# The order of the matmuls in the projection of a graph attention layer: block by block, or the blocks in turn

## The reference

```python
adj = dep_type_matrix != 0
dep_emb = dep_emb_table[dep_type_matrix]
hi_t = einsum('bid,de->bie', h, W1_w[:HID])[:, :, None, :] + einsum('bijd,de->bije', dep_emb, W1_w[HID:]) + W1_b
hj_t = einsum('bjd,de->bje', h, W2_w[:HID])[:, None, :, :] + einsum('bijd,de->bije', dep_emb, W2_w[HID:]) + W2_b
masked = where(adj, sum(hi_t * hj_t, axis=-1), NEG)
A = softmax(masked, axis=2)
h_syn = relu(einsum('bij,bjd->bid', A, h) @ gcn_w + gcn_b)
out = layernorm(x + h_syn @ Wo_w + Wo_b)
```

## Time and profile before

| | |
|---|---|
| time, median of 3 runs | 412.35 us (411.92 to 412.51) |
| span of the profiled execution | 410.8 us |
| PE busy | 397.4 us (97%) |
| PE, weight loads | 366.1 us (89%) |
| DVE busy | 319.2 us (78%) |
| POOL busy | 196.6 us (48%) |
| ACT busy | 130.8 us (32%) |
| DMA queue with the loads and stores | 33.9% of the 16 engines' time |

### The profile page before, as it was taken

How to read it: one execution, slowest core, us unless ns; L and a number is a source line. 1 busy time by engine, 2 the same in 40 slices (tenths; PEclk the granted TensorE clock), 3 DMA queues, 4 the chain that set the end, 5 groups by cost and what they waited for, 6 DMA issues and landing times.

```text
span 410.8 us, 8012 instructions
## 1 busy us (share of the span) xinstructions
PE 397.4 (97%) x2867; PEld 366.1 (89%) x2867; DVE 319.2 (78%) x640; ACT 130.8 (32%) x272; POOL 196.6 (48%) x159
## 2 busy tenths in 40 slices
PE   8999999999999999999999999999999999999971
PEld 4888998989999898999989899998989899898971
DVE  1544796988979698897979969697997979698764
ACT  1624233142323314232331333233142323314151
POOL 0290628165392816438173564717265292816052
PEclk9999999999999999999999999999999999999996
DMA  7903016070433507053070715216070342504022
GB/s 243 343 17 91 1 47 199 0 243 2 142 100 90 152 0 243 0 157 86 12 231 0 196 46 167 76 37 205 0 230 12 123 120 81 161 0 153 1 79 79
DMA packets 34476, 42.78 MB, mean 104 GB/s; under 512 B 9824, under 2 KB 28640, under 8 KB 34464
## 3 DMA queue, kind: packets, MB, share of 16 engines
q1 hardware_dynamic: 34320, 42.62, 33.9%
q10 hardware_dynamic: 144, 0.00, 0.0%
HBM read 30.03 MB, written 12.58 MB: 104 GB/s over the span
## 4 chain that ended last, share of the span: by engine, by line
PE 85%; DVE 9%; POOL 2%; issue 2%; DMA 1%; SPq 0%; DVEq 0%; POOLq 0%
PE bank L365 16%; PE bank L366 16%; PE bank L367 16%; PE bank L429 10%; PE bank L444 6%; PE bank L450 6%; PE bank L445 6%; PE bank L389 5%; DVE srow L763 2%; DVE rel L773 2%; PE bank L418 2%; PE bank L472 2%; DVE y_sb L696 1%; DVE stats L701 1%; DMA w1t_sb<-in_w_t_dram 1%
## 5 line engine op out<-in xcount | busy, mean ns | idle before, releaser
L971 POOL TENSOR_TENSOR veps<-mv,eps_sb 128x2 f32<-128x2 f32 (+1 forms) x33 | 8.6, 260 | 136.7 <-DVE mv L710 136.7
L688 DVE COPY hg_sb<-bank 128x385 f32<-128x385 f32 x64 | 35.6, 557 | 49.0 <-PE bank L367 47.2
L963 POOL TENSOR_TENSOR x_sb<-x_sb,wob_sb 128x1536 f32<-128x1536 f32 x16 | 58.3, 3648 | 28.5 <-DMA x_sb<-in_x_dram 28.5
L818 DVE CAST hs_hi<-hs_sb 128x512 fp32r<-128x512 f32 x48 | 66.6, 1412 | 1.8 <-ACT hs_sb L659 1.8
L444 PE MATMUL bank<-wo_hi,hs_hi 128*128 128x384 f32 x192 | 66.6, 347 | 0.0
L450 PE MATMUL bank<-wo_hi,hs_lo 128*128 128x384 f32 x192 | 65.2, 340 | 1.5 <-POOL hs_lo L1010 1.5
L365 PE MATMUL bank<-gcn_hi,xt_hi 128*128 128x386 f32 x192 | 66.5, 346 | 0.0
L445 PE MATMUL bank<-wo_lo,hs_hi 128*128 128x384 f32 x192 | 65.1, 339 | 0.0
L367 PE MATMUL bank<-gcn_hi,xt_lo 128*128 128x386 f32 x192 | 64.9, 338 | 0.0
L366 PE MATMUL bank<-gcn_lo,xt_hi 128*128 128x386 f32 x192 | 64.8, 338 | 0.0
L954 POOL TENSOR_TENSOR xt_lo<-xt_sb,xt_hi 128x1536 fp32r<-128x1536 f32 x15 | 52.2, 3483 | 16.2 <-ACT xt_hi L605 11.2
(11 more groups left out here) (77 smaller groups left out, 640.1 us busy)
## 6 DMA issues: line engine op xcount, KB each, us to landing
x_sb<-in_x_dram SPq DMA_DIRECT2D x16, 768.0 KB, 4.6
xt_sb<-in_x_t_dram SPq DMA_DIRECT2D x15, 768.0 KB, 5.5
out_dram<-y_sb SPq DMA_DIRECT2D x30, 384.0 KB, 3.4
adj_sb<-in_adj_dram SPq DMA_DIRECT2D x16, 128.0 KB, 5.2
xt_sb<-in_x_t_dram SPq DMA_DIRECT2D x2, 384.0 KB, 5.9
out_dram<-y_sb SPq DMA_DIRECT2D x4, 192.0 KB, 2.0
w2t_sb<-in_w_t_dram SPq DMA_DIRECT2D x3, 192.0 KB, 3.6
w1t_sb<-in_w_t_dram SPq DMA_DIRECT2D x3, 192.0 KB, 3.7
```

The source lines that it names most:

```text
L818: dve.tensor_copy(hs_hi[:, f, :], hs_sb[:, f, :]).then_inc(hshi, 1)
L963: pool.tensor_tensor(x_sb[:, slot], x_sb[:, slot], wob_sb[:].rearrange("p (o n) -> p o n", o=1).to_broadcast([P, PAIRS, HID]), ALU.add).th ...
```

## The change

In `proj` the block f becomes the innermost loop. All waits for `hg_ready` come ahead of the first matmul. Each of the three kinds of product (high-high, low x, low M) of a chunk c is done for the three blocks in turn, so that neighbouring matmuls write to banks 0, 1, 2, 0, 1, 2. The number of matmuls, their operands and sizes, and the order in which the terms of one block are added stay. The counts of `proj_mm` come with the last three matmuls.

```diff
@@ -369,14 +369,15 @@
             def proj(g, par):
                 pe.wait_ge(xlo, g + 1)
                 for f in range(C):
-
-
                     pe.wait_ge(hg_ready, PAIRS if isinstance(g, int) and g == 1 else PAIRS * g + min(f + 1, 2))
-                    fs = slice(f * P, (f + 1) * P)
-                    for c in range(C):
-                        mm = three(PROJ_BANK[f][:, 0:GT], m_hi[:, c, fs], m_lo[:, c, fs],
-                                   xt_hi[:, par, c, :], xt_lo[:, par, c, :], c == 0, c == C - 1)
-                    mm.then_inc(proj_mm, 1)
+                for c in range(C):
+                    for w, v in ((m_hi, xt_hi), (m_hi, xt_lo), (m_lo, xt_hi)):
+                        for f in range(C):
+                            mm = pe.matmul(PROJ_BANK[f][:, 0:GT], w[:, c, f * P:(f + 1) * P], v[:, par, c, :],
+                                           start=(c == 0 and w is m_hi and v is xt_hi),
+                                           stop=(c == C - 1 and w is m_lo))
+                            if c == C - 1 and w is m_lo:
+                                mm.then_inc(proj_mm, 1)
 
             def score_stage(g, par):
                 pe.wait_ge(gt_ready, C * (g + 1))
```

## The result

The changed kernel takes 431.93 us (430.66 to 432.42, 4 runs) against 412.3 for the kernel before, 1.045 times as long (95% interval 1.041 to 1.049). The prediction was 427.0 with a range of 418 to 432. The profiled execution spans 428.8 us.

The account below looks back on a forecast made before the run. PE, 97% busy, was taken as the bound, beside a second loop while `srow` is held. The start's 4.0 us and thirteen periods of 24.75 gave a span of 425.5; with 1.55 over the span, 427.0 us, range 418 to 432.

Parts of the forecast that it names:

- The matmuls: Projection matmuls on PE: changing bank neither gains nor costs, 0 taken, steps of 0.229 us.
- The head: Projection's first matmul waits for DVE's second `hg_sb` copy and starts at A + 5.77; PE waits 0.8 to 1.0 us.
- What is late next: After the head and tail: `srow` is held behind POOL's split in every group; period 24.75 us (24.5 to 25.1).
- A: The end of a group's second `attn` instruction on DVE, from which the prediction counts times.
- the lock: Held `srow` closes a second loop beside PE's, which PE cannot outrun: every group held, that loop's period 24.52 us.
- the forecast one over the normalisations, stores and load: Loop from A over DVE's normalisations, SP's stores, `xt` load, ACT's cast, POOL's split, `srow`, softmax: 24.52 us.
- The tail: Projection's end: three `gt_sb` evacuations come together, so value product 3 is 0.2 us late (0.1 to 0.4).
- The start: Once, at projection 0 and in the first body: 0.9 + 0.2 + 2.9 = 4.0 us later.
- The clock: Rival, first body: PE's clock falls to 1.2 GHz behind 2.7 us idle, 2 us more, 429; chance 0.11.
- A lock that slips: Rival, full groups: splits now and then begin late enough for `srow` to escape, 419 us at the limit; chance 0.17.
- the half clock in the projections: Rival: going round the banks puts PE at 1.2 GHz in the projections, 99 us more, 525; chance 0.01.
- shorter matmuls: Rival, projections: a matmul that changes bank gets shorter; at 60 ns each, 394 us; chance 0.03.

Follow-up runs that it names:

- alternate_two: The kernel before, with block 0 of the projection alone and blocks 1 and 2 alternating, without the wait at the head: 413.76 us, ratio 1.0022.
- act_srow: The changed kernel, with `srow` computed by ACT, between its cast and the exponentials, in place of DVE: 418.66 us, ratio 1.0122.
- copy_early: The changed kernel, with DVE's second `hg_sb` copy moved ahead of the first normalisation: 422.48 us, ratio 1.0264.
- waits_first: The kernel before, block by block, with only the wait for the second `hg_sb` copy moved ahead of the projection's first matmul: 420.29 us, ratio 1.0175.
- last_chunk_by_block: The changed kernel, with the last chunk's matmuls done block by block, so that the blocks end 0.69 us apart: 422.9 us, ratio 1.027.
- act_srow_exp_first: The changed kernel, with `srow` on ACT and the exponentials ahead of block 0's evacuation in the first body: 414.44 us, ratio 1.003.
- exp_first: The changed kernel, with ACT's exponentials of group 0 ahead of the evacuation of projection 1's block 0: 426.8 us, ratio 1.0356.
- srow_free: The changed kernel, with DVE's `srow` as a tensor_tensor with a broadcast operand in place of a tensor_scalar: 430.43 us, ratio 1.0425.
- before_srow_free: The kernel before, with DVE's `srow` as a tensor_tensor with a broadcast operand in place of a tensor_scalar: 412.43 us, ratio 0.9993.

## Why the prediction held, and where it was off

The time, 431.93, lies 0.07 us inside the range, and two of its four runs lie outside it: that the range held is luck. The forecast proper (427, 423 to 430) was too low, 14.7 us more where 19.6 came. What held is the kind of loss and most of its terms; the terms below say which were too small.

**The matmuls: right.** 0 was the value, 0.230 a step and alternate_two show it. One support was weaker than it looked: line 472 has 18 records for its 9 matmuls of M, so two records belong to one matmul and only every second of the 0.33 us steps changes the bank. The bound of a loss by that row is 0.02 a step, 8.6 us, and not 4. The 216 ns that the prediction takes from the Trainium skill (TensorE: Matmul & The Clock Gate, Back-to-back issue gap) are there the gap of an isolated matmul; for a stream of weight loads and matmuls, as here, the section has 131 ns at 512 columns. The steps of 230 ns fit neither.

**The head: right.** The projection starts 5.85 behind `attn` (117.00 against 111.15), forecast 5.77: the first matmul comes 0.14 behind the copy and not 0.06. PE's waits there add up to 10.2 us in 14 places, 0.7 each, where 0.8 to 1.0 were expected.

**What is late next: `srow` right, the path of the loop wrong in part.** `srow` is held in all thirteen groups. The period of thirteen groups is (384.81 - 61.40) / 13 = 24.88 from A to A, forecast 24.75 (24.5 to 25.1). act_srow shows that the lock, and not the wait alone, is the price; copy_early shows the escapes coming back. But the loop that sets the period isn't the forecast one over the normalisations, stores and load with 0.2 added: in twelve of the thirteen groups the cast follows the evacuations at once. The loop goes over PE and ACT. From A = 111.15 it is 5.85 to the projection, 6.02 to the first evacuation, 1.73 to the cast, 1.64 to the split, 3.48 for the split, and 6.07 from its end (`srow` is free, `rel`, softmax) to the next A: 24.79 in all. In every second group the split starts 0.30 behind the cast's end and not 0.16; so it did in the kernel before, and the forecast had taken a group with 0.16. Why the two differ is open.

The term that was too small is the start of the split. I had put the bunched evacuations at 0.2 us from one group. Between waits_first, without bunching (24.47 a group), and the changed kernel (24.81) lie 0.34, between last_chunk_by_block and it 0.42. In waits_first the cast starts between 12.85 behind A, when ACT is done with the evacuations, and 13.73, when the load comes late; in the changed kernel the busy ACT holds it at 13.6, and early landings gain nothing. The period was 0.13 longer than forecast: about half of it is the cast, at 13.60 where 13.33 + 0.2 was forecast, the other half the 0.30 of every second split. That is 13 x 0.13 = 1.7 us of the miss.

**The tail: right.** 0.17 us a group in act_srow_exp_first, forecast 0.2.

**The start: the mechanism right, one part left as a rival.** The transposes start at 41.92, 4.5 later than before, where 4.0 were forecast. The clock, given 0.11, did fall behind the idle time: the next two windows take 1.37 and 0.22 us longer, 1.6 in all, forecast at 2. A of group 1 is 61.40, 2.1 later than the sum had it. exp_first has neither the idle time nor the lower clock, and its first full group starts 4.1 sooner. The 1.6 us of clock don't come by themselves with the idle time, though: copy_early has the same 2.8 us and stays at 1.00.

**The sum.** +2.1 at the start, +1.7 in the periods, -0.5 at the end (28.45 for 29.0) give 428.8 for 425.5. The rest of the miss is outside the profile: the profiled run took 430.66, 1.9 over its span and the fastest of the four, and their median is 431.93.

**The rivals.** A lock that slips didn't come about: no full group of the changed kernel escaped. It came in copy_early. The clock in the first body did. Neither the half clock in the projections nor shorter matmuls appeared: the granted clock is 1.00 over all fourteen groups.

The 0.34 us that the bunched evacuations cost a group come over the cast and not over value product 3. Against waits_first the split starts 0.36 later behind A, 15.32 against 14.96 on average over the thirteen groups, which is the whole difference; and `srow`, which stands behind value product 3 and the score stage, begins ahead of the split's end in every one of them and is held to it. With `srow` on ACT value product 3 counts, 0.17. The idle time in the first body was forecast at 2.7 us and was 2.8.

## What to carry to other kernels

Making an accumulation loop go round several banks brought nothing here, but it moved things that looked like bookkeeping: all waits to the front, all completions to the end. Before turning such a loop inside out, ask which of its outputs someone takes early and which of its inputs someone delivers late. And look for a second loop beside the busiest engine's: a wait for another engine cost 0.7 us in each group only as long as that loop was closed, and moving one tiny instruction to another engine opened it. In the kernel before the same move saved 2.5 us.

## What the runs showed of the hardware

A DVE instruction of four columns, with all operands outside PSUM, was held until POOL's two-operand subtraction ended: 1.5 to 3.5 us instead of 0.23, as a tensor_scalar and as a tensor_tensor alike (204.86 against POOL's 204.84). I had expected the tensor_tensor to run free. On ACT the same work took 0.30 us beside the same POOL instruction. DVE's `rel`, which reads PSUM, ran at its usual pace beside the split: its eight instructions took 2.37 us from 120.05 in the kernel before, inside the split of the earlier trace rows, and 2.37 from 218.70, behind the split of the earlier trace rows. A larger instruction is held too: the third `hs_hi` cast, 128x512, took 3.76 us in the changed kernel, from 119.16, beside POOL's x plus bias from 118.95 to 122.63, and 3.76 in the kernel before; the median of these casts there is 0.42. Both ended 0.3 behind POOL's instruction. DVE then sits idle for 2.16 us until PE's next value product, so this costs nothing.

The Trainium skill (SBUF — State Buffer, Who interferes with whom) states that a DVE instruction with two inputs in SBUF contends with a GpSimd instruction that reads SBUF, as one in a 2-port mode does, and that whoever comes second is blocked to the end of the other's; ACT waits on no one. The rows agree on each point: both inputs of the tensor_tensor `srow` lie in SBUF, it was blocked to 204.86, and ACT's took 0.30. Read before the edit, the page would have told that srow_free and before_srow_free can't open the lock.

PE's granted clock fell during the work behind 2.8 us of idle time in the changed kernel, in act_srow and in srow_free. Behind the same 2.8 us in copy_early it stayed at 1.00, and so it did behind 1.9 us in last_chunk_by_block. So the idle time alone doesn't say whether the clock falls; what decides is open. The windows of the idle time and of the work behind it, first act_srow, then copy_early, then last_chunk_by_block:

```profile
40.10:42.91 2.81, 0.01 (x1) 0.04 (x1) 1.01 (x3) 2.71 (x11) 0.00 (x0) 1.00 0.00 0
42.91:46.30 3.39, 3.39 (x16) 3.39 (x17) 0.20 (x1) 0.59 (x1) 0.00 (x0) 0.64 0.02 5
```

```profile
39.73:42.56 2.83, 0.00 (x1) 0.03 (x1) 1.02 (x3) 2.73 (x11) 0.00 (x0) 1.00 0.00 0
42.56:44.58 2.02, 2.02 (x13) 2.02 (x14) 0.00 (x0) 0.59 (x1) 0.00 (x0) 1.00 0.03 8
```

```profile
39.36:41.27 1.91, 0.00 (x1) 0.03 (x1) 1.02 (x3) 1.82 (x7) 0.00 (x0) 1.00 0.00 0
41.27:43.29 2.02, 2.02 (x13) 2.02 (x14) 0.00 (x0) 0.59 (x1) 0.00 (x0) 1.00 0.03 8
```
